# V's weight rows in 32 transfers instead of 8, and the loads into ff_raw begun by GpSimd instead of the sync queue

## The reference

```python
def _L0_attn_ref(hidden_states, wq, bq, wk, bk, wv, bv, wl, bl):
    q = (hidden_states @ wq.T + bq).reshape(B, S, H, D)      # H = 32 heads, D = 32
    k = (hidden_states @ wk.T + bk).reshape(B, S, H, D)
    v = (hidden_states @ wv.T + bv).reshape(B, S, H, D)
    scores = jnp.einsum('bshd,bstd->bsht', q, k) / np.sqrt(D).astype(np.float32)
    probs = jax.nn.softmax(scores, axis=-1)
    return jnp.einsum('bsht,bstd->bshd', probs, v).reshape(B, S, E)

def _L0_ffn_ref(x, w1, w2, w3):
    dq1 = nf4_quant_dequant(w1)      # (2752, 1024): each block of 64 divided by its absmax,
    dq2 = nf4_quant_dequant(w2)      # rounded to one of 16 levels, multiplied again
    dq3 = nf4_quant_dequant(w3)      # (1024, 2752)
    gate = jnp.einsum('bsd,hd->bsh', x, dq1)
    up = jnp.einsum('bsd,hd->bsh', x, dq2)
    h = jax.nn.silu(gate) * up
    return jnp.einsum('bsh,dh->bsd', h, dq3)

x = x + _L0_attn_ref(_layernorm(x), ...)
x = x + _L0_ffn_ref(_layernorm(x), ...)
```

## Time and profile before

| | us |
|---|---|
| median of 3 runs | 2013.65 |
| lowest, highest | 2009.22, 2022.26 |
| profiled execution | 2010.74 |
| its span, first to last instruction | 2008.9 |

### The profile page before, as it was taken

One profiled execution on the slowest core, in us unless ns is written; L12 is line 12 of the kernel. 1 busy time (PEld: TensorE's weight loads), 2 busy tenths in 40 slices (PEclk: granted clock), 3 DMA queues, 4 the chain that ended last, 5 costly groups with the idle time before them and its releaser, 6 DMA issues. The chain is left out here.

```text
span 2008.9 us, 31136 instructions
## 1 busy us (share of the span) xinstructions
PE 1927.0 (96%) x10444; PEld 1072.8 (53%) x10444; DVE 1734.7 (86%) x1853; ACT 1480.3 (74%) x1672; POOL 1193.4 (59%) x715
## 2 busy tenths in 40 slices
PE   5699999999989899999999999999999999999998
PEld 5477887778766344444444444444444444444443
DVE  5468888777977899999989999899998999999992
ACT  5334353334457889989989899898998989998893
POOL 0111211111243678787887878878778797786975
PEclk8699999999999999999999999999999999999999
DMA  6235655655556633222121222212122221212114
GB/s 228 79 116 140 174 147 165 147 156 146 146 125 187 207 128 59 47 48 58 44 61 42 52 53 47 58 43 61 44 54 51 48 57 42 63 42 54 41 27 179
DMA packets 253358, 184.06 MB, mean 92 GB/s; under 512 B 177360, under 2 KB 220368, under 8 KB 253264
## 3 DMA queue, kind: packets, MB, share of 16 engines
q1 hardware_dynamic: 223696, 175.67, 31.4%
q10 hardware_dynamic: 29568, 7.34, 2.9%
HBM read 115.34 MB, written 25.17 MB: 70 GB/s over the span
## 5 line engine op out<-in xcount | busy, mean ns | idle before, releaser
L1489 ACT ACTIVATE signs<-w_nat,compare_bias 128x1024 int8<-128x1024 f32 (+2 forms) x896 | 958.9, 1132 | 16.9 <-issue 14.3
L1625 DVE SCALAR_TENSOR_TENSOR bank<-signs,bank 128x1024 f32<-128x1024 int8 (+2 forms) x761 | 926.5, 1218 | 47.7 <-ACT signs L1489 20.0
L1796 PE MATMUL bank<-x2T_hi,w12T_hi 128*128 128x512 f16 x1376 | 523.4, 380 | 9.2 <-DMA w12T_lo<-half 5.5
L1797 PE MATMUL bank<-x2T_lo,w12T_hi 128*128 128x512 f16 x1376 | 523.2, 380 | 0.0
L1798 PE MATMUL bank<-x2T_hi,w12T_lo 128*128 128x512 f16 x1376 | 523.0, 380 | 0.0
L1012 PE MATMUL bank<-wT_hi,xT_hi 128*128 128x512 f16 x768 | 294.9, 384 | 2.5 <-PEq L325 2.5
L1012 PE MATMUL bank<-wT_hi,xT_lo 128*128 128x512 f16 x768 | 294.7, 384 | 0.0
L1823 PE MATMUL bank<-w3T_hi,hT_hi 128*128 128x512 f16 x672 | 254.8, 379 | 8.0 <-DVE acc L1704 3.7
L1824 PE MATMUL bank<-w3T_lo,hT_hi 128*128 128x512 f16 x672 | 254.7, 379 | 0.0
L1825 PE MATMUL bank<-w3T_hi,hT_lo 128*128 128x512 f16 x672 | 254.7, 379 | 0.0
L1415 POOL TENSOR_TENSOR acc<-acc,hidden 128x512 f32<-128x512 f32 x176 | 221.3, 1273 | 34.1 <-ACT hidden L1538 33.3
(11 more groups left out here) (143 smaller groups left out, 2641.0 us busy)
## 6 DMA issues: line engine op xcount, KB each, us to landing
ff_raw<-in_L_ffn_w SPq DMA_DIRECT2D x63, 512.0 KB, 4.1
w_nat<-in_L_ffn_w SPq DMA_DIRECT2D x63, 512.0 KB, 3.7
x_nat<-in_L_attn_hidden_states SPq DMA_DIRECT2D x16, 512.0 KB, 3.9
x_res<-in_L_attn_hidden_states SPq DMA_DIRECT2D x16, 512.0 KB, 4.9
x<-x_res SPq DMA_DIRECT2D x16, 512.0 KB, 2.9
acc<-x SPq DMA_DIRECT2D x4, 2048.0 KB, 8.7
out<-acc SPq DMA_DIRECT2D x16, 512.0 KB, 2.7
w_raw<-in_L_attn_wq SPq DMA_DIRECT2D x8, 512.0 KB, 7.7
```

The source lines that it names most:

```text
L1489: nc.scalar.activation(signs[0:rows, ring(v, k), 0:cols], w_nat[0:rows, v % SLOTS, 0:cols], ACT.Sign, scale=COMPARE[SUMMED[k]][0], bias=co ...
L1625: V.scalar_tensor_tensor(to, part, HALF_STEP[SUMMED[k]], before, ALU.mult, ALU.add).then_inc(sign_used, 1)
L1796: nc.tensor.matmul(dst, hi, x2T_hi[:, toks, c], start=c == 0, stop=False)
L1797: nc.tensor.matmul(dst, hi, x2T_lo[:, toks, c], start=False, stop=False)
```

## The change

It has two parts.

The first is in the weight set-up. Each of V's eight loads becomes four, one for each 32 partitions, in the order 0, 2, 1, 3, on the same semaphore; `wait_part` waits for four times the count where the part is V's.

The second is in the attention steps. `load_ff` moves from the sync queue's program to GpSimd's. GpSimd's step begins the first load at its start, the second behind `inv_std`, the third behind `inv_std2`, the others behind `low2`. VectorE's places of looks become: at the start behind `turn_v`, behind `norm_apply`, behind `sum_rows`, behind the eviction of K's first half, and at the end. Steps 0, 1 and 14 have four looks each (three, three and six before). On the sync queue the step becomes store_x1, load_x, store_x2, load_res: load_res no longer waits for `low2` alone but stands behind store_x2, which waits for both transposes.

```diff
             def wait_part(eng, g, j):
-                eng.wait_ge(w_in[g // 2][g % 2 * GROUP_PARTS + j], 16)
+                eng.wait_ge(w_in[g // 2][g % 2 * GROUP_PARTS + j], 16 if g < 4 else 16 * (P // QUAD))
...
                 for k in range(LOADS):
-                    sp.dma_start(w_raw[2][:, k], by_dim[k]).then_inc(w_in[2][k], 16)
+                    for a in (0, 2, 1, 3):
+                        sp.dma_start(w_raw[2][a * QUAD:(a + 1) * QUAD, k], by_dim[k, a]).then_inc(w_in[2][k], 16)
...
         def sync(sp, feed):
-            def load_ff(tile, m, j, rows, slot, times, behind):
...
             def step(n, u, it, project=True, normalize=True, attend=True, end=True, feed=None):
-                todo = looks(n, u, it)
+                if end:
+                    store_x1(n - 2)
                 if normalize and not (it is None and n + 2 >= T):
                     sp.wait_ge(x_turned, 2 * n + 2)
                     load_x(sp, n + 2, u)
-                for look in todo[:1]:
-                    load_ff(*look)
-                if end:
-                    store_x1(n - 2)
                 if feed:
                     sp.wait_ge(projected, 6 * n + 2)
                     next(feed)
-                for look in todo[1:4]:
-                    load_ff(*look)
+                if end:
+                    sp.wait_ge(x2_turned, 32 * (n - 1))
+                    store_x2(n - 2)
                 if end and attend:
-                    sp.wait_ge(x2_lo_done, n - 1)
                     load_res(sp, n - 1)
...
-                for look in todo[4:]:
-                    load_ff(*look)
-                if end:
-                    store_x2(n - 2)
...
         def gpsimd(pool, feed):
+            def load_ff(tile, m, j, rows, slot, times, behind):
+                first = tile * P
+                pool.wait_ge(absmax_done, j + behind)
+                pool.sem_inc(held, 1)
+                if m < 2:
+                    pool.dma_start(ff_raw[0:rows, slot], (w1, w2)[m][bass.ds(first, rows), :]).then_inc(ff_in[slot], 16)
+                else:
+                    pool.dma_start(ff_raw[:, slot, 0:C * rows].rearrange("p (t h) -> p t h", t=C),
+                                 w3.rearrange("(t p) h -> p t h", p=P)[:, :, bass.ds(first, rows)]).then_inc(ff_in[slot], 16)
+
             def step(n, u, it, project=True, normalize=True, attend=True, end=True, feed=None):
+                todo = looks(n, u, it)
+                for look in todo[:1]:
+                    load_ff(*look)
                 if end:
                     residual(n - 2)
                 if normalize:
                     inv_std(pool, n + 1)
                 if it is None:
                     clear(n)
+                for look in todo[1:2]:
+                    load_ff(*look)
                 if end:
                     inv_std2(n - 2)
+                for look in todo[2:3]:
+                    load_ff(*look)
                 if feed:
                     next(feed)
                 if end:
                     low2(n - 2)
+                for look in todo[3:]:
+                    load_ff(*look)
...
                     turn_v(n)
+                look()
                 if normalize:
                     norm_stats(dve, n + 1, 1 - u, (n + 1) // 2 + 1 if it is None else it + 2 + u)
...
                     norm_apply(dve, n + 1, 1 - u)
+                look()
                 if attend:
                     flip_probs(n, 0, end)
-                look()
...
                                         qkv[:, 1].rearrange("p (h d) -> p h d", d=HD)).then_inc(k_ready, 1)
-                look()
                 if project:
                     evacuate(n, u, it, 2, 0)
-                look()
```

More of the change, by code:

```diff
@@ L587, in attention @@
         IN_LOOP = (5, 4)
-        assert FT == 2 + 3 * LOOP + 1 and REST
+        FIRST_LOOKS = 4
+        assert 3 * (FT + 1) == 3 * FIRST_LOOKS + 9 * LOOP and REST
         def looks(n, u, it):
@@ L593, in looks @@
                 places = [u * IN_LOOP[0] + k for k in range(IN_LOOP[u])]
-                return [(it * 3 + 2 + q // 3, q % 3, it * 9 + 6 + q, P, q % 2, it * (5, 4)[q % 2] + 3 + q // 2 + 1, 1 + (q == 0))
-                        for q in places]
+                return [(it * 3 + (2 * FIRST_LOOKS + q) // 3, (2 * FIRST_LOOKS + q) % 3, it * 9 + 2 * FIRST_LOOKS + q, P, q % 2,
+                         it * (5, 4)[q % 2] + FIRST_LOOKS + q // 2 + 1, 1 + (q == 0)) for q in places]
             if n < 2:
-                return [(j // 3, j % 3, j, P, j % 2, j // 2 + 1, 1) for j in range(3 * n, 3 * n + 3)]
-            first = 6 + 9 * LOOP
-            return [(j // 3, j % 3, j, P if j < 3 * FT else REST, (j + 1 - first) % 2, (5, 4)[(j + 1 - first) % 2] * LOOP + 3 + (j - first) // 2 + 1, 1)
-                    for j in range(first, first + 6)] if n == T - 2 else []
+                return [(j // 3, j % 3, j, P, j % 2, j // 2 + 1, 1) for j in range(FIRST_LOOKS * n, FIRST_LOOKS * (n + 1))]
+            first = 2 * FIRST_LOOKS + 9 * LOOP
+            return [(j // 3, j % 3, j, P if j < 3 * FT else REST, (j + 1 - first) % 2,
+                     (5, 4)[(j + 1 - first) % 2] * LOOP + FIRST_LOOKS + (j - first) // 2 + 1, 1)
+                    for j in range(first, first + FIRST_LOOKS)] if n == T - 2 else []
         def turn_high2(eng, n):
@@ L613, in sync @@
         def sync(sp, feed):
-            def load_ff(tile, m, j, rows, slot, times, behind):
-                first = tile * P
-                sp.wait_ge(absmax_done, j + behind)
-                if m == 2:
-                    sp.sem_inc(held, 1)
-                if m < 2:
-                    sp.dma_start(ff_raw[0:rows, slot], (w1, w2)[m][bass.ds(first, rows), :]).then_inc(ff_in[slot], 16)
-                else:
-                    sp.dma_start(ff_raw[:, slot, 0:C * rows].rearrange("p (t h) -> p t h", t=C),
-                                 w3.rearrange("(t p) h -> p t h", p=P)[:, :, bass.ds(first, rows)]).then_inc(ff_in[slot], 16)
             def step(n, u, it, project=True, normalize=True, attend=True, end=True, feed=None):
-                todo = looks(n, u, it)
+                if end:
+                    store_x1(n - 2)
                 if normalize and not (it is None and n + 2 >= T):
```

## The result

The changed kernel takes 2060.22 us (median of 4 runs, 2057.68 to 2065.22) against 2012.76 us before (4 runs, 2009.22 to 2022.26). The ratio is 1.0229, 95% interval [1.0194, 1.0264]: it is slower, 47 us in the medians, where 2 us faster was forecast and 2060 was the upper end of the range. The profiled execution has a span of 2057.1 us, 48.2 more than before.

What follows compares the result with a forecast made beforehand. TensorE was taken to set the pace, VectorE close behind. Set-up -24 us plus attention steps +21 gave -3: 2007.7 us profiled, 2011 as median; 8 in 10 from 1978 to 2060.

Steps and rivals of the forecast that it cites:

- Part 1: Weight set-up: V's 32 transfers use all sixteen transfer engines, so everything behind starts 24 us earlier (21 to 26).
- Rival E: Set-up: V's 32-row transfers still move at 104 GB/s, the 24 us are lost, 2035 us; chance 0.05.
- The fourth look: VectorE's check for the load begun behind low2: landing 5.2 us, waits 6.0 and 5.5, 11.5 us a pair of steps.
- rival C: Attention steps: GpSimd needs long to begin w3 loads of 1024 pieces; 2034 us at 2.7 us each, 2063 at 5; chance 0.20.
- The second look: VectorE's check for the load begun behind inv_std: a wait of 1.0 us a step, bounds 0 and 2.5.
- The pair: Two attention steps: 67.6 us in place of 64.6, VectorE setting the pace; 18 us over six pairs in the loop.
- The steps before and behind the loop: Attention steps outside the loop: about half a pair's price each, making the steps' loss 21 us in all.
- load_res at nothing: Residual load moved behind both transposes starts some 6 us later, hidden by the fourth look's wait; without that cover 14 us.
- The range: Whole kernel, 8 in 10: 1978 us to 2060 us (7 us landing, or w3 loads taking 4.8 us to begin).
- Rival D: VectorE's high-speed operations hold GpSimd off while it writes load descriptions: 3.2 us a pair, 21 in all, 2032; chance 0.05.
- Rival B: Attention steps: looks nearly hidden, landing at most 4.0 us at the fourth look; faster, down to 1967 us; chance 0.25.
- What was to show it: Trace signs: ff_raw waits of 90 to 110 us, pairs of 67 to 68 us, first projection at 68 us.

Runs made afterwards that it cites:

- e1: Kernel before with only V's loads split into 32 transfers and their waits: 1988.71 us, ratio 0.9876.
- e4: Changed kernel with all ff_raw loads at the same places but begun by the sync queue: 2018.90 us, ratio 1.0030.
- e14: e8 with the looks of steps 0 and 1 one place later: 1976.77 us, ratio 0.9807.
- e8: Changed kernel with GpSimd's fourth load ahead of low2 and load_res back at its old place: 1985.11 us, ratio 0.9852.
- e9: Changed kernel with load_res alone put back ahead of the wait for both transposes: 2072.98 us, ratio 1.0297.
- e3: Changed kernel with GpSimd's fourth load ahead of low2 instead of behind it: 2009.86 us, ratio 0.9981.
- e5: Changed kernel with the feed-forward tensors taken in the order w2, w3, w1, so w3's load changes place: 2057.91 us, ratio 1.0202.
- e6: Changed kernel with the fifth load of a five-load step begun only after VectorE's fourth look: 2067.67 us, ratio 1.0263.
- e13: Changed kernel with only the 22 w3 loads begun by the sync queue, at the same places: 2025.55 us, ratio 1.0053.
- e7: Changed kernel with ScalarE beginning the low half's transpose only after VectorE's fourth look: 2068.80 us, ratio 1.0258.

## Why the prediction was wrong, step by step

- **Part 1** was right. 24 us were taken, 21 to 26 the bounds; the trace gives 26.5 and e1 25. The step that chose the eviction of pair 16 gave 48.3, it came at 47.43. Its 416 GB/s did not hold for V's own loads, which move at 289 once they are alone, but ScalarE waits for none of them. Rival E is out.
- **The fourth look** is the step that failed, and in it one term: "I take 5.2" for the landing. For the five-load step the landing was 10.3 on average for 5.2, and the wait 11.0 to 11.9 for 6.0, outside the bounds of 3.2 and 8. For the four-load step 4.6 was measured for the landing, and a wait of 5.6 to 5.9 for 5.5; two small errors meet there, since VectorE arrives 1.1 us before low2's end and not 0.31 (0.81 was said for the other step, where it is 1.1 too). I took one landing for two different loads: the row was that of w1 and w2, and that the load behind low2 is w3's in every second step entered only rival C, as time to begin it.
- **The warning was in the trace before.** The maxima, 13.0 in the earlier trace rows and 13.3 in the earlier trace rows, are no strays: once in each pair the load beside the low half's transpose takes 10.6 to 13.0 us, and VectorE's 4.11 us of the earlier trace rows, which I only counted as something that goes away, are the wait for it. The bound should have been 13 and not 8.
- **The second look**: 1.0 a step was taken; it is 1.1 to 1.5 in one step of two and nothing in the other. Close.
- **The pair** by these: 67.6 forecast, 74.1 measured. Of the 6.5 between, 5.1 are w3's landing; the arrival ahead of low2 adds 1.1, w2's landing and the second looks take off 1.3, VectorE's short waits for its own results and ScalarE's add 1.2 and its own work takes off 0.8. That makes 5.3; 0.8 more is the measure, with six long steps among its eleven. e4, whose w3 load lands in 5.0, has 67.2: the rest of the step's sum was near enough.
- **The steps before and behind the loop** were costed at half a pair's price, 3 us in all, and cost 9.4 up to step 2 and some 10 behind step 13. Most of the first is a look that the change puts ahead of x's statistics in step 0, when its load is only just begun, 7.04 us; I had no row for it, and priced these steps by the loop. e14 shows its worth: 8 us against e8. The second was not taken apart; the very last look, of w3, waits 10 us there.
- **load_res at nothing** had the right cover and the wrong price. The cover that was named held: GpSimd waited 17.8 us for the rows, VectorE 0.6 us for the residual. But e9 shows what I had not thought of, that the move took a transfer out of the fourth load's way and was worth 13 us in this kernel. Without the cover it was put at a loss of 14 us; e3 against e8 says 25.
- **The range** ended at 2060 with two ways to it, and the measured 2060.22 lies just past that end. By the prediction's own sum one of them does not lead there: a landing of 7 us at both fourth looks adds 3.6 us a pair, 23 in all, and gives 2034; 2060 needs about 9. That the range nearly reached the result is therefore luck: it rested on rival C's 4.8 us to begin a w3 load, and beginning one took 0.94.
- **Rival C** had the right sign for the wrong reason. Beginning a w3 load takes GpSimd 0.94 us, 0.57 for the others; it needed 2.7 us to reach 2034. The Trainium skill, DMA: Bandwidth & Descriptors, section Anatomy of one DMA, calls the software's share of the time small, and these 0.94 us agree. The estimate of 3.2 us for a 512 KB load begun by GpSimd, worked out from the fit in that section, is below all of these loads: the shortest is 3.5, the medians are 4.6 and 5.6, and the one that mattered 10.3.
- **Rival D** is out at the place that counts: VectorE stands idle from 223.67 to 235.55 while the load is begun and on its way, so no operation of it can hold GpSimd off. **Rival B** needed a landing of 4.0 us in both steps; beside the transpose 4.1 is the best seen in the loop (e5), and that only for rows of 4 KB.
- **What was to show it** did: waits of 136.0 where 90 to 110 would have meant right, pairs of 74.1 where 67 to 68 would.

## What to carry to other kernels

A load's landing time is not a property of its size: before a load is put where an engine stands and waits for it, list for that very place which queue begins it, how many pieces it has, what other transfers are in flight and which of them is begun first, and keep a range as wide as the longest landing in the trace. Where the longest landings come back once in every turn, find out beside what. Start such loads ahead of the work that depends on something else (here low2, 50 us for one line of order). When a transfer is moved, ask both who waits for it and beside what it will run; putting load_res back cost 13 us or won 25, by what else was waiting.

## What the runs showed of the hardware

- A load of 1024 pieces of 512 bytes begun by GpSimd 0.16 us ahead of a DMA transpose lands after 9.8 to 10.6 us in the changed kernel's loop, and after 9.2 to 10.3 without a second load (e6). Begun by GpSimd 0.6 us behind the transpose it lands after 5.4 to 5.9 (e3); from the sync queue 0.3 us behind it in 5.0 (e4) to 6.8 (e13); without the transpose in 5.3 (e7); and with 128 pieces of 4 KB in its place in 4.3 (e5). So the order counts on GpSimd's queue; whether the queue counts beside it was not tried.
- Such a landing is not bound to w3 or to GpSimd: in the kernel before a load of 4 KB pieces from the sync queue lands after 10.6 to 13.0 us beside the transpose and the residual's load.
- The transpose suffers as well: 10.1 to 11.2 us beside GpSimd's w3 load, 10.6 to 13.3 in those steps of the kernel before, 3.1 to 5.0 where it is begun behind the look (e7). Why is open. The Trainium skill, DMA: Bandwidth & Descriptors, section SWDGE vs HWDGE vs iDMA, has each transfer engine go round between its inner queues, of which GpSimd's are other ones than the sync queue's; no run here shows whether that is the cause.
- GpSimd takes 0.57 us (median of 44) to begin a load of 128 rows and 0.94 us (median of 22) for one of 1024 pieces; the sync queue took 0.38 for the latter before the change.
- Splitting a transfer can halve its rate: V's loads, when alone, move at 104 GB/s with an outermost dimension of 4 and at 53 GB/s with 2; with 32 all sixteen engines work, at 289 GB/s.
